# A layer kernel on one core: ScalarE's square root and VectorE's first statistics moved to the head of each phase of the projection stage

## The reference

```
x = x + 0.5 * ffn(layernorm(x))        # mixture of 8 experts of rank 16, top 2 of 8 gates
x = x + attention(layernorm(x))        # 16 heads of width 16, relative positions
x = x + 0.5 * ffn(layernorm(x))        # the same weights

ffn(x):  logits = x @ Wg ; top 2 ; softmax over the two (an exp of their difference)
         out = sum over experts of gate * (x @ A[e]) @ B[e]
attention(w): q, k, v = w @ Wq.T, w @ Wk.T, w @ Wv.T ; rp = positions @ Wr.T
         score = ((q + u) k + rel_shift((q + v) rp)) / 4 ; out = softmax(score) @ v
layernorm(x): (x - mean) / sqrt(var + 1e-5)
```

## Time and profile before

| what | us |
|---|---|
| median of 3 runs | 2996.29 |
| profiled execution | 2993.58 |
| its span | 2991.8 |
| PE busy (TensorE) | 2862.4 (96%) |
| DVE busy (VectorE) | 2601.1 (87%) |
| ACT busy (ScalarE) | 2512.9 (84%) |
| POOL busy (GpSimd) | 2317.9 (77%) |

### The profile page before, as it was taken

How to read it: one execution, slowest core, us unless ns; L and a number is a source line. 1 busy time by engine, 2 the same in 40 slices (tenths; PEclk the granted TensorE clock), 3 DMA queues, 4 the chain that set the end, 5 groups by cost and what they waited for, 6 DMA issues and landing times.

```text
span 2991.8 us, 101339 instructions
## 1 busy us (share of the span) xinstructions
PE 2862.4 (96%) x40768; PEld 2022.3 (68%) x40768; DVE 2601.1 (87%) x5002; ACT 2512.9 (84%) x3878; POOL 2317.9 (77%) x4151
## 2 busy tenths in 40 slices
PE   6885999999999999999999999999999999999986
PEld 3651777776777777777777777777777777777756
DVE  5871999899998999999998999999999999999977
ACT  4555998898998998898898988988988988889962
POOL 4557888888788888888788888888888888888850
PEclk8995999999999999999999999999999999999998
DMA  6578788888888888888888888888888888888771
GB/s 228 174 211 217 210 226 230 223 226 233 223 228 230 222 232 226 223 229 229 220 234 224 226 235 221 229 229 226 227 231 224 227 231 229 227 227 222 210 202 57
DMA packets 290228, 656.76 MB, mean 220 GB/s; under 512 B 189536, under 2 KB 256992, under 8 KB 272352
## 3 DMA queue, kind: packets, MB, share of 16 engines
q0 software_dynamic: 190960, 526.89, 66.7%
q1 hardware_dynamic: 98800, 123.38, 13.9%
HBM read 77.19 MB, written 46.14 MB: 41 GB/s over the span
## 4 chain that ended last, share of the span: by engine, by line
PE 86%; POOL 4%; DVE 3%; ACT 3%; DMA 3%; issue 2%; DVEq 0%; SPq 0%; ACTq 0%; POOLq 0%
PE pt_bank L1094 29%; PE acc_bank L1108 19%; PE ac_bank L1080 17%; PE pos_bank L1028 14%; POOL score L896 3%; PE pos_bank L1066 3%; DMA score<-score 2%; PE bank_one L477 1%; ACT score L1155 1%; PE bank_one L262 1%; PE bank_two L262 0%; DVE rest L619 0%; PE bank_one L448 0%; PE bank_two L251 0%; DVE normed_one L152 0%
## 5 line engine op out<-in xcount | busy, mean ns | idle before, releaser
L896 POOL DMA_DIRECT2D score<-score x3999 | 2178.3, 548 | 464.9 <-ACT score L1157 396.3
L1155 ACT COPY score<-pos_bank 128x512 f32<-128x512 f32 x2048 | 1104.1, 597 | 241.3 <-PE pos_bank L1028 239.6
L1165 ACT ACTIVATE score<-score,low 128x1024 f32<-128x1024 f32 x1024 | 1197.9, 1170 | 32.9 <-DVE low L1225 32.9
L1234 DVE COPY prob_t<-pt_bank 128x512 f32<-128x512 f32 x1768 | 1146.8, 683 | 3.6 <-PE pt_bank L1094 3.6
L1094 PEld LDWEIGHTS pt_bank<-ident_sb,score 128*128 128x128 f32 x8192 | 946.6, 142 | 211.7 <-issue 118.1
L1094 PE MATMUL pt_bank<-ident_sb,score 128*128 128x128 f32 x8192 | 1078.1, 274 | 4.3 <-ACT prob_t L1173 1.2
L1225 DVE CUSTOM_DVE_ANT_0 score<-ac_bank,score 128x1024 f32<-128x1024 f32 x512 | 627.0, 1225 | 243.2 <-PE ac_bank L1080 120.5
L1225 DVE CUSTOM_DVE_ANT_0 score<-ac_bank,score,low 128x1024 f32<-128x1024 f32 x512 | 657.2, 1284 | 47.2 <-PE ac_bank L1080 37.6
L1108 PE MATMUL acc_bank<-prob_t,vs 128*32 128x128 f32 x16384 | 659.6, 279 | 0.0
L1028 PE MATMUL pos_bank<-pos,qv 96*32 96x512 bf16 (+15 forms) x12160 | 655.3, 316 | 3.8 <-ACT score L1155 2.5
L1080 PE MATMUL ac_bank<-ks,qu 96*128 96x512 bf16 x2048 | 622.3, 386 | 36.6 <-DVE low L1225 35.9
(11 more groups left out here) (97 smaller groups left out, 847.7 us busy)
## 6 DMA issues: line engine op xcount, KB each, us to landing
score<-score POOLq DMA_DIRECT2D x3937, 129.5 KB, 5.1
pos<-pos_parts SPq DMA_DIRECT2D x96, 128.0 KB, 8.6
qv<-qv_parts SPq DMA_DIRECT2D x192, 64.0 KB, 7.3
ks<-k_parts SPq DMA_DIRECT2D x192, 64.0 KB, 7.3
qu<-qu_parts SPq DMA_DIRECT2D x192, 64.0 KB, 7.3
v_heads<-v_sb SPq DMA_DIRECT2D x8, 1024.0 KB, 6.1
vs<-v_heads SPq DMA_DIRECT2D x32, 256.0 KB, 8.1
pos_parts<-part SPq DMA_DIRECT2D x16, 384.0 KB, 2.7
```

Source lines behind the costliest of these rows:

```text
L896: pool.dma_start(shifted(odd, s, groups, 0), shifted(odd, s, groups, QUAD - 1 - s))\
L1155: act.copy(score[:, at + f, c * BANK:(c + 1) * BANK], ring(m)[:, :]).then_inc(pos_out, 1)
L1165: act.activation(cols, cols, ACT.Exp, bias=low[:, slot(k), NH - 1:NH], scale=-1.0)\
L1234: dve.tensor_copy(prob_t[:, c, :], PT[c % 2][:, :]).then_inc(copied, 1)
```

## The change

ScalarE: the square root for the ahead norm is a step of its own at the head of b's work, taken between the copies of a's transposed norm and a's `Exp`. It stood behind the copy of a's gated hidden layer. VectorE: the ahead norm's statistics and variance come first in the phase, ahead of a's gates; its reciprocal and normalizing come right behind the gates, ahead of rest 0; and the rests 4 and 5 stand between the variance and the reciprocal of a's second norm instead of behind that norm. No instruction is added or removed, and TensorE, GpSimd and SyncE keep their orders.

```
@@ ScalarE, project(lane, n)
                     B, S = LB[lane], LS[lane]
+                    if n + 1 < ROUNDS:
+                        root(act, B, S, 2 * n + 3)
+                    yield
                     for kt in range(KT):
...
                     taken(1)
                     yield
-                    if n + 1 < ROUNDS:
-                        root(act, B, S, 2 * n + 3)
                     for j in (1, 2, 3):
@@ ScalarE, order(first, second)
-                    for which in (first, first, second, second, first, second, first, second):
+                    for which in (first, second, first, second, second, first, second, first, second):
@@ VectorE, order(a, b)
+                    next(ahead, None)
+                    next(ahead, None)
                     for _ in range(GATE_STEPS):
                         next(up, None)
-                    next(ahead, None)
-                    next(ahead, None)
-                    next(rest)
                     finish(ahead)
-                    for _ in range(3):
+                    for _ in range(4):
                         next(rest)
                     finish(up)
+                    next(after, None)
+                    next(after, None)
+                    finish(rest)
                     finish(after)
-                    finish(rest)
```

## The result

The changed kernel takes 3015.99 us in the median of four runs (3013.68 to 3020.06), the kernel before 2996.70 us in four (2993.58 to 2998.78). The ratio is 1.0065, with a 95% interval of 1.0050 to 1.0081: **slower by 19.3 us, 15 to 24 us by the interval**. The forecast was slower by 10.5 us, 3007 us, in a range of 2988 to 3014. Direction and mechanism came as forecast; the size lies outside the range.

The account below looks back on a forecast made before the run. It took a chain, no full engine, to bound stage one. A longer path, +3.7 us at full clock, and TensorE's lower clock, +6.8, made +10.5 on 2996.29: 3007 us, range 2988 to 3014.

Parts of the forecast that it names:

- What goes: Before x_one: table load, root and ahead normalizing leave the path, 1.5 us won; p is the Q projections' start.
- VectorE's path: Behind the second norm's variance: rests, reciprocal and normalizing take 5.8 us beside GpSimd's backlog, bounds 2.9 and 5.8.
- ScalarE's path: Behind the ahead variance: root 0.25 us, then the Exp table load, 0.1 + 1.28 us, no longer in idle time.
- The phase at full clock: Stage one, from one Q projection start to the next: 22.2 us, against 20.90 before.
- the clock: TensorE's Q projections after some 3.5 us idle: lower clock in four or more of seven, 6.8 us, bounds 0 and 11.9.
- The base: The kernel before's first trace, stage two starting at 224.52 us, used as reference for the full-clock sum.
- stage one's loss is passed on one to one: From stage one to the program's end: whatever stage one gains or loses counts fully in the total time.
- Rival 1: In stage one VectorE and GpSimd pass each other freely, so the kernel gets faster: 2989 us, chance 0.15.
- Rival 2: No change: TensorE's clock holds, or GpSimd's backlog is half as long: 2998 to 3000 us, chance 0.25.
- Rival 3: Change hidden because stage two's start hangs on a store of stage one: 2996 us, chance 0.03.

Follow-up runs that it names:

- the run with GpSimd held: The changed kernel with one added wait: GpSimd starts the parts of rest 4 only when a's second norm is done; 2995.17 us, ratio 1.0000.
- the first experiment: The changed kernel with rests 4 and 5 back behind a's second norm, early statistics and square root kept; 2990.45 us, ratio 0.9976 to the kernel before.
- with filler: The changed kernel with 20 identity transposes, results unread, in TensorE's idle time before the Q projections of phases one to seven; 3008.33 us, ratio 1.0038.
- the second pair of traces: Both kernels, unedited, profiled once more: 2996.30 us for the kernel before, 3012.24 us for the changed one.
- statistics-alone run: The kernel before with only VectorE's ahead statistics and variance moved ahead of the gates, ScalarE's order as before; 3007.59 us, ratio 1.0036.
- the root in the gap: The kernel before with the ahead root behind part 4 and VectorE's ahead reciprocal and normalizing behind the second norm's variance; 2997.74 us, ratio 0.9996.

## Why the prediction was right in kind and short in size

- *What goes.* Right. In the run with GpSimd held x_one starts at 138.01, p + 8.43 with p = 129.58, the very 8.43 read from the seventh phase; the ahead norm did fit into idle time.
- *VectorE's path.* Right: 5.8 us were taken for rests, reciprocal and norm; the chain has 2.24 + 0.2 + 3.58 = 6.0. That GpSimd's work is the cause is shown by the held run, that the two take turns by the ends of their instructions.
- *ScalarE's path.* Right in place: root, table load and `Exp` follow one another at 135.21, 135.44 and 136.73. The drain of 1.38 us for a switch, of which the Trainium skill tells in "ScalarE: Activation LUTs", section "What ACT_TABLE_LOAD costs", does not show: from the load's start to `Exp` it is 1.29 us. That this load is a cost of its own was too strongly put: in the first experiment it stands there too, and the kernel gains.
- *The phase at full clock.* 22.2 us forecast, 22.25 to 22.35 with filler.
- *The step that failed: the clock.* It was put as "four or more of the seven later projections: 4 x 1.7 = 6.8 us (bounds 0 and 7 x 1.7 = 11.9)". In the trace six of the seven ran low, and 1.7 was too small a unit: the excess over 3.70 us is 3.07, 2.63, 2.37, 1.70, 2.44 and, in the eighth phase, 1.82 with 0.9 more in its transposes, 14.9 us in all, above the upper bound. The two slow projections of the earlier trace rows had followed idle times of 2.0 us and were at the lower level for a part of their length only (granted clock 0.68 over each, against 0.54 over the 6.77 us); 1.7 was no bound for what follows 3.4 us. I had the long gap in the text and priced it by rows of a short one. The sum of the trace then closes: 16.7 = 14.9 of clock + 1.8 for everything else, where 3.7 was forecast, the first phase's 1.7 of clock among them, which did not come. Not all of the 14.9 would be won back by a full clock: slow projections give GpSimd room ahead of the rests, so that x_one comes at p + 10.26 - 2.37 = 7.89 instead of 8.43, and the filler returned about 8, with the eighth phase still slow. (The eight instructions of 5.40 and 3.70 us are both Q products; the prediction calls them the Q and first K product. No number changes by it.)
- *The base.* The first trace of before had stage two at 224.52, the second at 221.03. My sum stood on the one with 3.5 us more in it, part of which was its own low clock in L262. The 2.6 us between the 16.7 of the traces and the 19.3 of the medians are not explained by that alone: the profiled execution of the changed kernel, 3010.06, is 5.9 us under its median, that of before 3.1 under its own, and the second pair of traces is 18.9 us apart at the start of stage two but only 15.9 in time. That stage one's loss is passed on one to one held for the first pair (16.7 and 16.5); single executions differ by more in stage two, see the last section. The cause of that part stays open.
- *The rivals.* Rival 1 (VectorE and GpSimd pass freely) is false here. Rival 2 (the clock holds) is false, and would not have sufficed: with filler the kernel is still 0.38% slower. Rival 3 is false.

## What to carry to other kernels

Where two engines hold each other up, put the instructions that feed the second behind those of the first that are on the path: two rests in front of a norm cost 10 us, and 26 us where they undid the gain of the other half of the change. Holding the second engine back took away the loss (ratio 1.0000), but moving the rests was better (0.9976). Bound what an idle gap of TensorE costs by the whole of the work that follows it, not by the slow rows of a shorter gap, and take the clock of the kernel before out of the base. Look at the last phase by itself: nothing there hid the delay. Try the halves of a change apart: one half of this one, kept, is 7 us faster than before.

## What the runs showed of the hardware that was not expected

The lower clock after 3.42 us of idle time came in all ten of the phases two to six of two traces. The gap in front does not decide it alone. Two Q projections of the run with GpSimd held, and one of the kernel before with the rests ahead of the norm:

```profile
150.21 3.70 PE L477 MATMUL bank_one<-normed_t_one,wq_sb 128*128 128x512 f32 x8 [3.10 <-ACT normed_t_one L546]
...
170.84 5.40 PE L477 MATMUL bank_one<-normed_t_one,wq_sb 128*128 128x512 f32 x8 [3.10 <-ACT normed_t_one L546]
```

```profile
87.97 5.40 PE L477 MATMUL bank_one<-normed_t_one,wq_sb 128*128 128x512 f32 x8 [0.94 <-ACT normed_t_one L543]
```

The same 3.10 us of idle time are followed by full and by lower clock, and the lower clock also comes after 0.94 us. The statistics-alone run has a Q of 3.70 us behind 3.28. So the length of one gap gives a risk and no forecast; what else decides was not tested.

Stage two is not as even as I took it. From its first product to the end of the span it took 2767.3 and 2773.5 us in the two traces of before and 2767.1 and 2770.4 in those of the changed kernel, but 2775.8 to 2776.9 in the first experiment, the one with the root in the gap and the one with the statistics alone, and 2770.2 to 2773.4 in the six others, with no instruction of it changed. In single executions this hides or adds up to 10 us beside what stage one gains or loses; of its cause nothing was tried.
